# Rounding h in seven of eight chunks on ScalarE, in the first 13 blocks of an MoE FFN

## The reference

```python
out = einsum('bsi,io->bso', Efou * ys[:, None, :], weight) * d[:, None, :]
logits = einsum('bsd,de->bse', input_emb, Wr) + br
route_w = softmax(logits); _, topk_idx = top_k(route_w, 2)
routed = route_w * mask; routed = routed / routed.sum(-1, keepdims=True)
h = relu(einsum('bsd,edh->ebsh', input_emb, W1) + b1[:, None, None, :])
expert_out = einsum('ebsh,ehd->ebsd', h, W2) + b2[:, None, None, :]
x = x + einsum('bse,ebsd->bsd', routed, expert_out)
```

## Time and profile before

| | |
|---|---|
| median of 3 runs | 947.36 us (947.02 to 948.51) |
| the profiled execution's own time | 945.56 us |
| its span, from first to last instruction | 943.7 us |
| mean granted TensorE clock | 0.984 of full |
| busy: TensorE 95%, VectorE 79%, ScalarE 61%, GpSimd 50% | of the span |

### The profile page before, as it was taken

One profiled execution on the slowest core, in us unless ns is written; L12 is line 12 of the kernel. 1 busy time (PEld: TensorE's weight loads), 2 busy tenths in 40 slices (PEclk: granted clock), 3 DMA queues, 4 the chain that ended last, 5 costly groups with the idle time before them and its releaser, 6 DMA issues.

```text
span 943.7 us, 20861 instructions
## 1 busy us (share of the span) xinstructions
PE 899.6 (95%) x6454; PEld 887.0 (94%) x6454; DVE 741.6 (79%) x1431; ACT 571.4 (61%) x991; POOL 472.4 (50%) x445
## 2 busy tenths in 40 slices
PE   5975989999999999999999999999999999999995
PEld 5954989999999999999999999999999999999995
DVE  4793769889888777887887878878878878878874
ACT  6744656678876666556556556556556556556562
POOL 6953254445445255545545545545545555545553
PEclk9997989999999999999999999999999999999998
DMA  7594875945354353423434234234234234234222
GB/s 246 212 346 147 321 203 124 269 101 111 73 134 86 73 141 85 89 51 85 89 96 89 45 90 89 46 89 92 48 84 95 47 82 95 51 80 93 51 39 28
DMA packets 52214, 104.24 MB, mean 110 GB/s; under 512 B 7120, under 2 KB 34288, under 8 KB 51536
## 3 DMA queue, kind: packets, MB, share of 16 engines
q0 software_dynamic: 27360, 38.36, 24.2%
q1 hardware_dynamic: 20688, 61.09, 19.5%
q10 hardware_dynamic: 4128, 4.33, 1.4%
HBM read 75.78 MB, written 36.35 MB: 119 GB/s over the span
## 4 chain that ended last, share of the span: by engine, by line
PE 84%; DMA 7%; DVE 4%; issue 2%; ACT 1%; POOL 1%; SPq 0%; POOLq 0%; ACTq 0%; DVEq 0%
PE psum L1509 13%; PE psum L1511 13%; PE psum L1510 13%; PE psum L1524 13%; PE psum L1522 13%; PE psum L1523 13%; DMA out<-in_x 2%; PE psum L1488 2%; DMA x_buf<-in_xT 2%; PE psum L1386 1%; PE psum L1401 1%; PE psum L1402 1%; PE psum L1403 1%; DVE h_lo L1320 1%; DMA raw<-in_xT 1%
## 5 line engine op out<-in xcount | busy, mean ns | idle before, releaser
L824 ACT ACTIVATE h<-psum,b_all 128x384 f32<-128x384 f32 x376 | 217.6, 579 | 279.2 <-PE psum L1511 222.8
L1522 PE MATMUL psum<-w_hi,h_hi 128*128 128x256 f32 x1128 | 319.2, 283 | 1.4 <-DVE h_lo L1320 1.4
L1524 PE MATMUL psum<-w_hi,h_lo 128*128 128x256 f32 x1128 | 319.2, 283 | 0.0
L1523 PE MATMUL psum<-w_lo,h_hi 128*128 128x256 f32 x1128 | 318.9, 283 | 0.0
L1509 PE MATMUL psum<-z_hi,w_hi 128*128 128x384 f32 x752 | 259.2, 345 | 5.6 <-ACT h L824 3.4
L1268 DVE TENSOR_TENSOR w_lo<-raw,w_hi 128x1024 fp32r<-128x1024 f32 x190 | 232.2, 1223 | 29.6 <-ACT w_hi L761 26.8
L1510 PE MATMUL psum<-z_lo,w_hi 128*128 128x384 f32 x752 | 254.7, 339 | 0.0
L1511 PE MATMUL psum<-z_hi,w_lo 128*128 128x384 f32 x752 | 254.5, 338 | 0.0
L1320 DVE TENSOR_TENSOR h_lo<-h,h_hi 128x384 fp32r<-128x384 f32 x376 | 210.9, 561 | 22.6 <-ACT h L824 9.4
L761 ACT ACTIVATE w_hi<-raw 128x1024 fp32r<-128x1024 f32 x190 | 200.6, 1056 | 28.1 <-PE psum L1524 20.4
L1522 PEld LDWEIGHTS psum<-w_hi,h_hi 128*128 128x128 f32 x1128 | 213.9, 190 | 2.4 <-DVE h_lo L1320 2.2
(11 more groups left out here) (212 smaller groups left out, 731.8 us busy)
## 6 DMA issues: line engine op xcount, KB each, us to landing
raw<-in_experts SPq DMA_DIRECT2D x64, 512.0 KB, 4.5
x_buf<-in_xT SPq DMA_DIRECT2D x12, 512.0 KB, 9.2
z_rows<-z_all ACTq DMA_DIRECT2D x2, 2112.0 KB
d_rep<-d_rows SPq DMA_DIRECT2D x3, 1056.0 KB, 9.1
z_rows<-z_all SPq DMA_DIRECT2D x1, 2112.0 KB, 8.6
z_rows<-z_once SPq DMA_DIRECT2D x1, 2112.0 KB, 14.0
raw<-in_xT SPq DMA_DIRECT2D x4, 512.0 KB, 9.5
z_row<-z_rows,idx_get POOLq DMA_INDIRECT x99
```

Source lines behind the costliest of these rows:

```text
L824: act.activation(h[c % NHP][:], h_ps[c % HP][:, 0:TB], ACT.Relu, bias=b1_all[:, ds(e, 1), c]).then_inc(s_relu, 1)
L1522: pe.matmul(yp, hi, w2(w_hi, c), start=(c == 0), stop=False)
L1523: pe.matmul(yp, hi, w2(w_lo, c), start=False, stop=False)
L1524: ins = pe.matmul(yp, lo, w2(w_hi, c), start=False, stop=(c == HC - 1))
```

## The change

The rounding of `h` into `h_hi` moves from VectorE to ScalarE for chunks 1, 2, 4 and 5 of blocks 0 to 12, beside chunks 3, 6 and 7, where it was already. That is 52 roundings. Chunk 0 stays on VectorE. The second hunk leaves out a wait for buffers that have never been used in block 0, and the third adjusts the count by which VectorE's own semaphore steps.

```diff
-    ACT_HI = (3, 6, 7)
+    ACT_HI = (1, 2, 3, 4, 5, 6, 7)
...
                     if act_hi(b, c):
-                        act.wait_ge(s_h2, b * HC + c + 1 - NHX)
+                        if not (fresh and c < NHX):
+                            act.wait_ge(s_h2, b * HC + c + 1 - NHX)
                         act.activation(h_hi[c % NHX][:], h_ps[c % HP][:, 0:TB], ACT.Relu,
                                        bias=b1_all[:, ds(e, 1), c]).then_inc(s_hhi_act, 1)
                     act.activation(h[c % NHP][:], h_ps[c % HP][:, 0:TB], ACT.Relu,
...
             def block_of_dve(b, fresh):
-                given = sum(act_hi(b - 1, c) for c in (HC - 2, HC - 1)) if isinstance(b, int) and b >= 1 else 0
+                given = sum(act_hi(b - 1, c) for c in range(1, HC)) if isinstance(b, int) and b >= 1 else 0
```

## The result

The changed kernel takes 951.19 us (median of 8 runs, 949.53 to 954.81) against 947.58 us (8 runs). The ratio is 1.0039, with a 95% interval of 1.0021 to 1.0056. The forecast was 950.0 us in a range of 947.2 to 952.2.

A forecast was written before the change was run, and what follows sets the result against it. TensorE, busy 95% of the span, was taken to set the pace. Losses of 0.47 + 1.1 + 0.7 + 0.4 = 2.7 us, less 0.1 for freed VectorE, took 947.36 to 950.0 us, range 947.2 to 952.2.

The forecast's parts named there:

- What bounds the kernel, and what there was to gain: Block 2's second half to block 9: TensorE waits at most 2.3 us for VectorE in 139 us.
- the step that counted VectorE's part of the waits at 0.1 us: Blocks 2 to 9: of the 2.3 us TensorE waits for VectorE, only 0.1 us counted as gained.
- The price, 0.47 us: Every moved rounding: ScalarE pays 0.47 us, since successive activations overlap; four in a block make 1.88 us.
- Ordinary blocks at nothing: Blocks 0, 2 to 5, 7, 10 to 12: no cost; without the cover of TensorE's matmuls, up to 1.88 us each.
- Block 1, 0.47 us: Block 1, chunk 5, behind a late weight piece: `h_hi` delays F(7) by 0.47 us; bounds 0.24 and 0.47.
- Block 9, 1.1 us: Block 9: ScalarE has no idle time to chunk 6, so F(6) comes 1.1 us late; bounds 0 and 1.5.
- Block 6, 0.7 us: Block 6 into 7: late `z_hi` delays `z_lo` and block 7's F(0) by 0.7 us; bounds 0.3 and 1.2.
- Block 8, 0.4 us: Block 8 into 9: 1.88 us less ScalarE's idle time leaves 0.4 us at block 9's F(0); bounds 0 and 0.8.
- The sum: Blocks 1, 9, 6 and 8 together cost 2.7 us, less 0.1 for freed VectorE; the median rises by 2.6 us.
- the one in which VectorE was the late one: Ends of blocks 2 to 8, at `h_lo` and `z_lo`: kernel gets faster by 2.3 us, 945.1 us; chance 0.07.
- The one that ScalarE's delays pass from block to block: Blocks 5 to 9: ScalarE becomes the bound, some 1 us each beyond the sum in four blocks, 954; chance 0.11.

The follow-up runs named there:

- late chunks: Kernel before, with ScalarE also rounding chunks 4 and 5 in block 3, 5 in block 6, 4 in block 9; 947.90 us, one timing.
- mix: Kernel before, with chunk 5 of block 6 also rounded on ScalarE and all eight chunks of block 7 on VectorE; 946.91 us, ratio 0.9986.
- none on ScalarE: Against the kernel before, VectorE rounds all eight chunks in blocks 0 to 12 and ScalarE none; ratio 1.0036 (1.0021 to 1.0051).
- early-chunks run: Kernel before, with chunks 1 and 2 also rounded on ScalarE in blocks 3, 6 and 9; 949.09 us, one timing.
- The experiment on `r_next`: Changed kernel, with VectorE copying `r_next` of block 3 after chunk 2 instead of chunk 3; 948.28 us, one timing; block 3 takes 18.66 us.

## Why the prediction was right, and where it was not

**What bounds the kernel, and what there was to gain.** Right: TensorE sets the pace, and relief of VectorE brought nothing in total. But the step that counted VectorE's part of the waits at 0.1 us was wrong in block 6, and in block 1 (below). The cast of chunk 5 was on the path there; moved alone, it gains 0.4 us (late chunks, mix). The whole change hides this gain behind ScalarE's delay. The opposite experiment, none on ScalarE, shows how little room VectorE had: it lost 3.4 us. Block 6 is the case that "Perfetto Trace Analysis" of the Trainium skill (section "Optimizing Scalar/DVE Operations") describes, in which it can pay to move work off a saturated VectorE. I set the rule aside by the share over the whole span, 79%; it holds at the end of block 6, where VectorE's rows have no idle time.

**The price, 0.47 us.** Right: 130.56 to 131.02 and 279.52 to 279.98 in the rows above, 0.46 us. The estimate of 0.507 us that I worked out from "ScalarE: Activation LUTs" of the Trainium skill (section "What ACT_TABLE_LOAD costs") is 0.04 to 0.05 too high here. The sum with it was also misreckoned: the price enters once in block 1, but three times in block 9, five times in block 6 and at least four times in block 8, so it comes to some 3.2 us and not 2.9.

**Ordinary blocks at nothing.** Right for 2, 4, 5, 7 and 10 to 12: each is within 0.06 us of before or within the scatter of its two profiles. Block 0 varies from 19.0 to 20.3 us in either kernel and tells nothing. Wrong for block 3, and this is the step that failed: 19.25 to 19.39 us in place of 18.62 to 18.79, some 0.65 us. I followed the added roundings to `h` and to TensorE, and not through VectorE to `r_next`, which frees the row buffer for GpSimd's gather. By the early-chunks run chunks 1 and 2 alone cost half of it; chunks 4 and 5 alone cost nothing. `h_lo` of chunk 3 waits for ScalarE, `w_lo` and `r_next` stand behind it, the gather begins 0.45 us later after the block's first F, and it falls together with ScalarE's DMA issue. The experiment on `r_next` took the loss away.

**Block 1, 0.47 us.** Right in its place: 1.58 us became 2.04. From F(7) to block 2's F(0) it is 5.75 to 5.91 us in the five profiles in which ScalarE rounds all seven chunks of block 1. Of the seven others, four have 5.97 to 6.06, so 0.1 to 0.2 us come back. The clock does not explain it: the mean granted clock over this stretch is 0.71 to 0.73 in all nine. But in each of the four, and in none of the five, TensorE's weight load for the second product of chunk 5 waits 0.25 to 0.5 us for `h_lo`, which stands behind VectorE's cast. The row from the second profile of before:

```profile
134.14 0.29 PEld L1522 LDWEIGHTS psum<-w_hi,h_hi 128*128 128x128 f32 x1 [0.25 <-DVE h_lo L1320]
```

So what comes back is, as far as the rows show, VectorE's relief; no experiment tried it alone. The remaining three profiles (before, none, mix) take 6.6 to 7.1 us, and there the mean clock is 0.56 to 0.62. In the first profile of before it was at 0.50 for all of the 6.1 us behind F(7); in the changed kernel it was at 0.71 on the average:

```profile
131.60:137.50 5.90, 5.86 (x33) 5.86 (x34) 5.05 (x10) 3.69 (x7) 4.68 (x5) 0.71 0.77 156
```

(Stretch, its length, busy time of TensorE, its weight loads, VectorE, ScalarE and GpSimd, clock, DMA share, GB/s.) So this block varies from one execution to the next by more than the change does to it.

**Block 9, 1.1 us.** Measured 1.0. Chunks and places were right: the wait is at F(6) for `h` of chunk 4, goes away when work ahead of it is moved, and has a threshold. Two terms were off and partly cancelled: the room ahead of F(6) was 0.57 us and not 0.35 (chunk 0's `h` came 0.28 us earlier than in the kernel before), and F(6) took 0.14 us to start behind `h`, not 0.05. The row of F(6) shows a wait of 0.73 us, where some 1 us was forecast.

**Block 6, 0.7 us.** Measured 0.65, by the step that was named: `z_hi` late, `z_lo` waiting. `z_lo` starts 18.57 us after the block's F(0) in place of 17.93, 0.64 later where 0.74 was reckoned.

**Block 8, 0.4 us.** Measured 0.25 in four profiles of five; mis-sized by 0.15. In the fifth, the first of the changed kernel, `h` of chunk 7 came another 0.6 us later and the block took 0.7 us more; no other profile shows that.

**The sum.** With 0.3 for block 1, 0.65, 0.25, 1.0 and 0.65 for block 3 it is 2.85 us; the two timings of the changed kernel say 3.7 and 2.7 us (ratios 1.0039 and 1.0029, each uncertain by 1.6). That the forecast of 2.6 lies so near is in part luck: the four blocks that it charged with 2.7 us cost 2.2, and block 3, charged with nothing, cost the 0.65 that made up for it. Of the rivals, the one in which VectorE was the late one holds for chunk 5 of block 6, and for the small gain in block 1. The one that ScalarE's delays pass from block to block is not seen: no block after 9 is longer, and 4, 5 and 7 are as before.

## What to carry to other kernels

Work that is moved between two engines with room on the average costs in the few places where the taking engine has a queue without idle time. Read there, instruction by instruction, how far each result comes ahead of the one that waits for it, and add the moved time up to that point. Then follow the delayed result through the other engine too, to whatever buffer it frees: the missed 0.65 us came from a gather that started only 0.45 us later. Choose by place: three roundings fewer in one block and one more in another beat the rule that treats all blocks alike, by 0.8 us in the trace, which the timing is too coarse to confirm.

## What was not expected of the hardware

A DMA issue on ScalarE's queue took longer when GpSimd's third gather no longer started clearly ahead of it. In the six profiles where the gathers kept their place that gather started 0.29 to 0.47 us ahead of L778's second issue, and the issue took 2.34 to 2.57 us; where they were moved much earlier it took 2.36. With the gathers 0.45 us later, the third started 0.07 us ahead in the early-chunks kernel, where the issue took 2.74 us, and 0.20 to 0.21 us behind in the other four profiles, where it took 2.96 to 3.10.

That the two overlap is not enough. With the late chunks they did so for 1.6 us, by the records, and the issue took 2.42:

```profile
169.17 1.87 POOL L577 DMA_INDIRECT z_row<-z_rows,idx_early  x1 [0.30 <-issue]
...
169.46 2.42 ACTq L778 DMA_DIRECT2D z_rows<-z_all  x1
```

ScalarE did not start its next activation meanwhile: `h_hi` of chunk 7 starts 0.22 us after the issue has ended in the kernel before and in the changed one alike. Which resource the two share was not tried.
